# A graph and mixer network on one core: the second graph layer's projection in two column passes, with the attention columns in the first

## What is computed

```
xn = layernorm(x)
x  = x + gat2(elu(gat1(xn))) + mixer(xn)     # mixer ends in out @ proj_w.T + proj_b
x  = x + moe(layernorm(x))
```

```
h    = h1 @ W2                      # (1250 x 2048) @ (2048 x 768)
al_s = h . att_src2, al_d = h . att_dst2      # one number per node each
e    = leaky_relu(al_s[src] + al_d[dst]);  m = segment_max(e, dst)
ex   = exp(e - m[dst]);  out = segment_sum(h[src] * ex) / segment_sum(ex) + bias
```

## Time and profile before

| what | us |
|---|---|
| median of three runs | 2380.92 |
| the profiled execution | 2381.91 |
| its span, first to last instruction | 2380.1 |
| PE busy (88% of the span) | 2089.4 |
| DVE busy | 1112.9 |
| ACT busy | 414.8 |
| POOL busy | 202.4 |
| matmuls of the second layer's projection (L1337, x640) | 209.2 |
| mean granted TensorE clock | 0.927 |

### The profile page before, as it was taken

One profiled execution on the slowest core, in us unless ns is written; L12 is line 12 of the kernel. 1 busy time (PEld: TensorE's weight loads), 2 busy tenths in 40 slices (PEclk: granted clock), 3 DMA queues, 4 the chain that ended last, 5 costly groups with the idle time before them and its releaser, 6 DMA issues. The chain is left out here.

```text
span 2380.1 us, 33762 instructions
## 1 busy us (share of the span) xinstructions
PE 2089.4 (88%) x9786; PEld 1453.8 (61%) x9787; DVE 1112.9 (47%) x2372; ACT 414.8 (17%) x743; POOL 202.4 (9%) x197
## 2 busy tenths in 40 slices
PE   4998999889799994399999979975985799999997
PEld 2666666644345553288888845543554577777776
DVE  4113212422566665788888700117646333333433
ACT  1222121200011113122222200000000122222221
POOL 0000000000000001000000000000001123333322
PEclk9998999889899995599999989997996799999999
DMA  7002200142200007623333241182116488899664
GB/s 224 0 0 70 90 0 0 42 102 71 93 24 22 24 22 261 201 95 121 116 100 99 66 179 50 52 199 73 53 35 235 117 244 253 263 278 283 185 147 78
DMA packets 73572, 271.79 MB, mean 114 GB/s; under 512 B 10230, under 2 KB 26682, under 8 KB 63911
## 3 DMA queue, kind: packets, MB, share of 16 engines
q1 hardware_dynamic: 52263, 204.94, 26.3%
q0 software_dynamic: 14688, 54.19, 9.8%
q10 hardware_dynamic: 6560, 11.86, 1.3%
HBM read 208.95 MB, written 62.00 MB: 114 GB/s over the span
## 5 line engine op out<-in xcount | busy, mean ns | idle before, releaser
L1187 PE MATMUL gat_Z<-h,gat_wt 125*125 125x256 f32 (+1 forms) x1600 | 354.2, 380 | 20.5 <-DVE gat_wt L1103 20.5
L1187 PEld LDWEIGHTS gat_Z<-h,gat_wt 125*125 125x125 f32 x1600 | 297.6, 188 | 65.7 <-DVE gat_wt L1103 21.0
L552 PE MATMUL mix_G<-mix_w,mix_xs 128*125 128x384 f32 x720 | 243.5, 489 | 0.0
L835 PE MATMUL count_G<-gnn_w,xnT 128*125 (+1 forms) x480 | 214.8, 597 | 17.0 <-issue 17.0
L2004 PE MATMUL ex_PH<-ex_xT,ex_w 128*128 128x128 f32 x1872 | 224.0, 279 | 2.4 <-issue 0.9
L1337 PE MATMUL gat2p_Y<-gat2p_w,gat2p_hT 128*125 128x384 f32 x640 | 209.2, 491 | 12.1 <-DMA gat2p_w<-in_L_gnn_W 12.1
L2004 PEld LDWEIGHTS ex_PH<-ex_xT,ex_w 128*128 128x128 f32 x1872 | 215.0, 193 | 3.7 <-issue 3.7
L2014 PE MATMUL ex_PY<-ex_w,ex_hT 128*128 128x384 f32 x624 | 214.7, 494 | 1.2 <-ACT ex_hT L1953 1.0
L552 PEld LDWEIGHTS mix_G<-mix_w,mix_xs 128*125 128x125 f32 x720 | 133.4, 189 | 85.4 <-issue 3.1
L1337 PEld LDWEIGHTS gat2p_Y<-gat2p_w,gat2p_hT 128*125 128x125 f32 x640 | 121.3, 190 | 99.7 <-issue 14.8
L2014 PEld LDWEIGHTS ex_PY<-ex_w,ex_hT 128*128 128x128 f32 x624 | 114.3, 190 | 77.4 <-ACT ex_hT L1953 3.1
(11 more groups left out here) (291 smaller groups left out, 2321.7 us busy)
## 6 DMA issues: line engine op xcount, KB each, us to landing
ex_w<-in_L_ffn_W SPq DMA_DIRECT2D x64, 1152.0 KB, 9.1
gat_cnt<-c_dram SPq DMA_DIRECT2D x50, 546.9 KB
h1T_dram<-gat_oT ACTq DMA_DIRECT2D x40, 250.0 KB, 2.0
gat2p_hT<-h1T_dram SPq DMA_DIRECT2D x10, 1000.0 KB, 4.8
mix_w<-in_L_mix_qkv_w SPq DMA_DIRECT2D x6, 1152.0 KB, 12.5
ct_dram<-count_out SPq DMA_DIRECT2D x40, 157.0 KB, 2.1
mix_w_slice<-in_L_gnn_W SPq DMA_DIRECT2D x6, 1024.0 KB, 10.9
gat2p_w<-in_L_gnn_W SPq DMA_DIRECT2D x4, 1536.0 KB, 13.6
```

The costliest lines, as they stand in the source:

```text
L552: last = pe.matmul(G[c][:], xs[b][:, k, :], w[:, k, c, :], start=(k == 0), stop=(k == KD - 1))
L835: last = pe.matmul(G[t % 2][:], xnT[:, k, t * P:(t + 1) * P], w[:, k, bass.ds(hd * C1, C1)], start=(k == 0), stop=(k == KD - 1))
L1187: last = pe.matmul(Z[b][j][:], wt[b][:, s, :], h[:, s, bass.ds(hd, 1), j * HC:(j + 1) * HC + j], start=(s == 0), stop=(s == NT - 1))
```

## The change

In the output projection, SP loads, behind x, the two attention rows of the second layer and all of W2 (6144 KB, in four chunks) into their own tiles; DVE's loop is unrolled, and from tile 2 on DVE makes, after the copy for the tile two further on, four multiply-and-accumulates of 768 columns: two rows of 128 of W2 times the two attention vectors, 32 in all, into wa2 (128 x 16 x 2).

In the second layer's projection POOL copies wa2 into columns 384 and 385 of each of the 16 blocks of the weight tile. The work is 20 half-tiles, q = 0 to 19: first columns 0 to 385 for all ten tiles of nodes, then the other 384 columns for all ten. The tiles of h1T are thus loaded twice. W2 is loaded in eight chunks of 768 KB (1536 bytes per row), the four of the second pass one by one with the loads of q = 2 to 5; the mask is loaded tile by tile with q = 2 to 11, and x1 with q = 12. DVE evacuates the whole first pass, and al2 is a copy of two columns. ACT evacuates the second pass. The chain is woven in: PE transposes al2 after q = 10, and m after q = 15 (MAX_AT = 5). ACT, no longer SP, stores alT, waits for it, loads the two rows, and stores m. No loop is left in this phase.

```
+    a2_loaded, wa2_step = cx.sem("proj_a2_loaded"), cx.sem("proj_wa2_step")
+        w2s = sb(nc, st, "proj_w2s", [128, KF, D])
             rows_dma(sp, xr, x.rearrange("(t p) d -> p t d", p=P), x_loaded)
+            sp.dma_start(a2[:, 0, :], a_src2[0, :].partition_broadcast(128)).then_inc(a2_loaded, 16)
+            sp.dma_start(a2[:, 1, :], a_dst2[0, :].partition_broadcast(128)).then_inc(a2_loaded, 16)
+            for c in range(KF // KC):
+                sp.dma_start(w2s[:, c * KC:(c + 1) * KC, :],
+                             W2[c * KC * 128:(c + 1) * KC * 128, :].rearrange("(k p) n -> p k n", p=128)
+                             ).then_inc(w2_loaded[c], 16)
...
+            def attention_columns(k):
+                if k % KC == 0:
+                    dve.wait_ge(w2_loaded[k // KC], 16)
+                if k == 0:
+                    dve.wait_ge(a2_loaded, 32)
+                for s in range(2):
+                    n = 2 * k + s
+                    if n >= 2:
+                        dve.wait_ge(wa2_step, n - 1)
+                    dve.tensor_tensor_reduce(out=junk[:, s, :], in0=w2s[:, k, :], in1=a2[:, s, :], scale=1.0,
+                                             scalar=0.0, op0=ALU.mult, op1=ALU.add,
+                                             accum_out=wa2[:, k, s:s + 1]).then_inc(wa2_step, 1)
+
+            for t in range(NT):
+                add(t)
+                if t + 2 < NT:
+                    turn(t + 2, t % 2)
+                if t >= 2:
+                    for k in range(2 * (t - 2), 2 * (t - 1)):
+                        attention_columns(k)
...
+            load_h(0)
             for c in range(KF // KC):
+                load_w(0, c)
+            load_h(1)
+            for q in range(2, 2 * NT):
+                sp.wait_ge(projected, q - 1)
+                load_h(q)
+                if q - 2 < KF // KC:
+                    load_w(1, q - 2)
+                if q - 2 < NT:
+                    rows_dma(sp, mask[:, q - 2, :], mask_dram[q - 2, :, :], mask_loaded)
+                elif q - 2 == NT:
+                    rows_dma(sp, x1, x1_dram.rearrange("(t p) d -> p t d", p=P), x_loaded)
+
+        @block.gpsimd
+        def _(pool):
+            pool.tensor_copy(w[:, :, HW:W], wa2[:]).then_inc(ext_ready, 1)
...
             for t in range(NT):
+                dve.wait_ge(projected, t + 1)
+                dve.tensor_copy(h2[:, t, 0:HW], Y[t % 2][0][:, 0:HW]).then_inc(ev_first, 1)
+                dve.tensor_copy(al2[:, t, :], Y[t % 2][0][:, HW:W]).then_inc(ev_first, 1)
...
+            def evacuate(t):
+                act.wait_ge(projected, NT + t + 1)
+                act.activation(h2[:, t, HW:D], Y[t % 2][1][:, 0:HW], ACT.Copy).then_inc(ev_second, 1)
+
+            evacuate(0)
+            act.wait_ge(copied, 3)
+            act.dma_start(al2T_dram, alT[:]).then_inc(stored, 16)
+            act.wait_ge(stored, 16)
+            act.dma_start(row[:], al2T_dram[0, :].partition_broadcast(128)).then_inc(row_loaded, 16)
+            act.dma_start(rows_t[:], al2T_dram[1, :].partition_broadcast(128)).then_inc(rows_loaded, 16)
+            for t in range(1, MAX_AT + 1):
+                evacuate(t)
+            act.wait_ge(m_copied, 3)
+            act.dma_start(m2T_dram, mT[:]).then_inc(m_stored, 16)
+            for t in range(MAX_AT + 1, NT):
+                evacuate(t)
+            act.wait_ge(m_stored, 16)
...
+            def project(q):
+                t, j = q % NT, q // NT
+                b = t % 2
+                pe.wait_ge(in_loaded[q % 2], q // 2 * 16 + 16)
+                if t >= 2:
+                    pe.wait_ge(ev_second if j else ev_first, t - 1 if j else 2 * (t - 1))
+                cols = slice(j * W, j * W + HW) if j else slice(0, W)
                 for c in range(KF // KC):
+                    if t == 0:
+                        pe.wait_ge(w_loaded[j][c], 16)
+                    for k in range(c * KC, (c + 1) * KC):
+                        last = pe.matmul(Y[b][j][:, 0:HW if j else W], hT[q % 2][:, k, :], w[:, k, cols],
+                                         start=(k == 0), stop=(k == KF - 1))
                 last.then_inc(projected, 1)
 
+            pe.wait_ge(ext_ready, 1)
+            for q in range(NT + 1):
+                project(q)
+            pe.wait_ge(ev_first, 2 * NT)
             for j in range(3):
                 for t in range(width[j]):
                     last = pe.transpose(T[j][:, t, :], al2[:, 4 * j + t, :], ident[0:P, 0:P])
                 last.then_inc(turned, 1)
+            for q in range(NT + 1, NT + MAX_AT + 1):
+                project(q)
+            pe.wait_ge(copied, 3)
             pe.wait_ge(m_ready, 1)
...
+            for q in range(NT + MAX_AT + 1, 2 * NT):
+                project(q)
```

More of the change, by code:

```diff
@@ L310, in proj_phase @@
     biased = cx.sem("proj_biased")
+    a2_loaded, wa2_step = cx.sem("proj_a2_loaded"), cx.sem("proj_wa2_step")
+    KC = 4
+    w2_loaded = [cx.sem(f"proj_w2_loaded{c}") for c in range(KF // KC)]
     with ExitStack() as st:
+        w2s = sb(nc, st, "proj_w2s", [128, KF, D])
+        a2 = sb(nc, st, "proj_a2", [128, 2, D])
+        junk = sb(nc, st, "proj_junk", [128, 2, D])
         bias = sb(nc, st, "proj_bias", [128, 2, D])
@@ L1225, in gat2_project_phase @@
     dve_step = cx.sem("gat2m_step")
-    w_loaded = [cx.sem(f"gat2p_w{c}") for c in range(KF // KC)]
+    w_loaded = [[cx.sem(f"gat2p_w{j}{c}") for c in range(KF // KC)] for j in range(2)]
     in_loaded = [cx.sem(f"gat2p_in{b}") for b in range(2)]
-    HW = D // 2
     with ExitStack() as st:
-        w = sb(nc, st, "gat2p_w", [128, KF, D])
-        ab = sb(nc, st, "gat2p_a", [128, 2, D])
-        junk = sb(nc, st, "gat2p_junk", [P, 2, D])
+        w = sb(nc, st, "gat2p_w", [128, KF, D + 2])
+        junk = sb(nc, st, "gat2p_junk", [P, N])
         hT = [sb(nc, st, f"gat2p_hT{b}", [128, KF, P]) for b in range(2)]
@@ L1239, in gat2_project_phase @@
         mT = sb(nc, st, "gat2p_mT", [1, N])
-        Y = [[pb(nc, st, f"gat2p_Y{b}{j}", [P, HW]) for j in range(2)] for b in range(2)]
+        Y = [[pb(nc, st, f"gat2p_Y{b}{j}", [P, W]) for j in range(2)] for b in range(2)]
         T = [pb(nc, st, f"gat2p_T{j}", [2, 4, P]) for j in range(3)]
@@ L1256, in _ @@
[L1256 to L1272, removed]
+            def load_h(q):
+                sp.dma_start(hT[q % 2][:], h1T_dram[q % NT, :, :].rearrange("p (f d) -> p f d", d=P)
+                             ).then_inc(in_loaded[q % 2], 16)
@@ L1304, in _ @@
                     dve.wait_ge(maxed, t)
-                dve.tensor_tensor_reduce(out=mjunk, in0=row[0:P, :], in1=mask[:, t, :], scale=1.0, scalar=-3.0e38,
+                dve.tensor_tensor_reduce(out=junk[:], in0=row[0:P, :], in1=mask[:, t, :], scale=1.0, scalar=-3.0e38,
                                          op0=ALU.subtract, op1=ALU.max, accum_out=big[:, t:t + 1]).then_inc(maxed, 1)
             dve.wait_ge(maxed, NT)
+            dve.wait_ge(ev_first, 2 * NT)
             step(dve.tensor_tensor(big[:], big[:], al2[:, :, 1], ALU.add))
@@ L1324, in _ @@
+            for t in range(MAX_AT + 1, NT):
+                evacuate(t)
+            act.wait_ge(m_stored, 16)
         @block.tensor
         def _(pe):
[L1326 to L1331, removed]
-                for c in range(KF // KC):
[L1333 to L1338, removed]
-                last.then_inc(projected, 1)
@@ L1341, in _ @@
[L1341 to L1345, removed]
-            pe.wait_ge(al_step, 2 * NT)
+            def project(q):
[5 more added lines that the diff above has]
+                cols = slice(j * W, j * W + HW) if j else slice(0, W)
+                for c in range(KF // KC):
+                    if t == 0:
[3 more added lines that the diff above has]
+                                         start=(k == 0), stop=(k == KF - 1))
+                last.then_inc(projected, 1)
```

58 lines of the change are left out of this document (19 added, 39 removed).

## The result

| | before | after |
|---|---|---|
| median (lowest to highest) | 2384.1 (2375.8 to 2401.9) | 2375.3 (2354.7 to 2383.6) |
| runs | 20 | 20 |
| profiled execution, span | 2381.9, 2380.1 | 2375.3, 2373.5 |

The ratio of after to before is 0.9924, with a 95% interval of 0.9904 to 0.9943: faster by 0.76%, some 18 us. The means differ by 16.2 us (2387.6, 2371.4), the medians by 8.8. These don't agree because neither kernel has one time. Of the 20 runs after, 7 lie at 2354.7 to 2365.8 (median 2360.3) and 13 at 2373.9 to 2383.6 (2376.2); of the 20 before, 14 at 2375.8 to 2389.2 (2383.8) and 6 at 2395.8 to 2401.9 (2397.4). Upper group against upper group the change brings 21 us, lower against lower 24. The forecast, 2355.0 with a range of 2346 to 2364, had the direction right; the time is 20 us above it and outside its range.

What follows compares the result with a forecast made beforehand. PE, busy 88% of the span, was taken as the bound, with gaps around the second projection. Terms -32.6 - 1.5 + 0.5 + 5.5 + 1.5 + 0.6 = -26.0 us gave 2355, range 2346 to 2364.

Steps and rivals of the forecast that it cites:

- PE's clock doesn't enter: Start of the aggregation: PE meets it after 10.5 us idle instead of 11.9, so no clock term was added.
- end gap: Between the second projection's last matmul and the aggregation: hiding the chain cuts 45.57 us of gap, saving 32.6 us.
- start: Start of the second projection: a smaller first chunk of W2 lets PE begin earlier, -1.5 us.
- two columns: Two extra columns in the first pass's matmuls and the aggregation's first half: 0.5 us, plus 0 for the loads, taken +0.5.
- wait for tile 13: First pass, q = 13: h1T's tile 13 queues behind x1, PE waits 1.3 to 9.4 us, taken +5.5.
- clock behind it: After the wait at q = 13, PE's clock drops and the next instructions run slower, +1.5 us.
- output projection: End of the output projection: DVE's last reductions delay the logits, +0.6 us (0 to 3.6); x's wait unchanged.
- B: Rival, second projection: x1 is not in the way, tile 13 lands in time; -33 us, 2348; chance 0.22.
- D: Rival: reading h1T twice makes loads bound both passes, slower than before, 2415 at 130 GB/s; chance 0.05.
- P: Rival, output projection: x shares bandwidth evenly with W2 and comes 9.4 us later, 2364; chance 0.06.
- a wait for x above 11 us: Sign that would prove the forecast wrong: PE's wait for x in the output projection, then 10.79 us, growing.
- C: Rival, second projection: the first pass waits for loads at q = 2 to 5, 8 us, 2363; chance 0.12.

Runs made afterwards that it cites:

- e5: Changed kernel with ACT's store of al2 and its broadcast row loads moved behind the evacuations of tiles 0 to 2; 2358.5 us, one run.
- e1: Kernel before with ten spare matmuls filling PE's idle time ahead of the norm-and-routing phase; 2385.6 us, ratio 0.9976.
- e7: Changed kernel with SP waiting for x in the output projection before loading the attention rows and W2; 2373.7 us, one run.
- e8: Changed kernel with the whole chain (both transposes, ACT's store and loads) behind the last half-tile, so not hidden; 2391.4 us, one run.
- e9: Changed kernel with x1 loaded by tile, W2 loaded only after x has landed, reductions one tile earlier; 2348.7 us, ratio 0.9824.
- e2: Changed kernel with the same ten spare matmuls as e1 ahead of the norm; 2368.3 us, ratio 0.9901.
- e10: Same three edits on the changed kernel as e9, plus the ten spare matmuls of e1; 2344.9 us, ratio 0.9818.
- e6: Changed kernel with only x1's last 13 partitions loaded two tiles later, with q = 14; 2357.8 us, one run.

## Why the prediction was wrong

**The step that failed** is the sum itself: its six terms are all of the touched phases, and every other phase stands in it at nothing, without a reason. "Nothing outside these phases is touched" was taken to mean that nothing outside them moves; "PE's clock doesn't enter" was said of the aggregation alone, and no sentence asks for the clock of the norm. I summed the change against one execution of before and took it to be the same kernel in all else. Its norm phase had its clock back at 1.00 after some 3 us; that of the profiled execution after never had: +13.6 us, the largest term of the difference after the hidden chain. That such a price was possible could have been read before the change: the trace of before has the norm's first matmuls at 0.50, behind 8.6 us of idle time. The three times given for before (2379.93 to 2384.01) all lie in its lower group, so nothing shown had the second one. They were also low within it: the 20 runs of before have a median of 2384.1, 3.2 us above the 2380.9 that I started from.

**The difference of the profiled spans**, 2373.5 - 2380.1 = -6.6, adds up: start of the output projection -1.5 (473.1 against 474.6; from 100 to 220 us the mean granted clock is 0.94 before and 0.99 after), output projection +3.0, up to the second projection -0.4, its start -1.8, projection -20.9, aggregation +1.5, norm +13.6, the rest -0.1. The touched phases bring -19.7 where I had -26.0. Term by term (the six add up to -19.1; 0.6 us are not placed):

| term | forecast | measured | from |
|---|---|---|---|
| end gap | -32.6 | -32.1 | PE idle 10.99, not 10.51 |
| start | -1.5 | -1.8 | 7.21 us from load to matmul, was 9.00 |
| two columns | +0.5 | +0.5 | tile to tile 10.37 us in the first pass, 10.32 in the second |
| wait for tile 13 | +5.5 | +9.4 | 9.42 |
| clock behind it | +1.5 | +1.9 | 12.40 - 10.32 - 0.17 |
| output projection | +0.6 | +3.0 | below |

**The wait** was the right mechanism at the wrong size, at the very end of its bounds (1.3 to 9.4). I had the rows at 0 to 5.6 us, and e5 shows 4.8. Without them the sum left 1.3 to 3.8 us, and e5 still waits 4.6: x1, taken at the mean of its first load, has a piece of 13 partitions that I had not priced apart, and issuing it later takes 5.9 us off. On the rule that the DMA engines take turns between queues ("DMA: Bandwidth & Descriptors", "Queues, rings and completion order", in the Trainium skill) the trace agrees: ACT's small store landed 5.9 us after its issue while x1's 3.84 MB were still moving in SP's queue, both rows landed before tile 13, and taking the rows out of that time took 4.8 us off the wait. B (tile 13 in time) and D are out.

**The output projection** is P in small. x doesn't keep its place ahead of W2, but what it loses is not half the bandwidth: PE restarts 27.6 us after the phase's first load, not 25.9, and the wait is 12.5 against 10.8 (+1.7), the 24 matmuls behind it 10.31 against 9.44 (+0.9), and the reductions at the end, from the last add's end to the logits, 581.86 - 578.04 = 3.8 against 3.4 (+0.4; the prediction's own times, 580.9 and 580.41, give +0.5, not +0.6). The sign that I had named, a wait for x above 11 us, came true, but it was a poor one: e1 has 12.0 without any load of W2 there. I took 0 from a load of x whose followers behind it I counted as proof; that row had no run without them to stand against. e7 takes away 2.9 of the 3.0.

**Right by the runs:** m's transposes in their slot (no wait of PE there), ACT's and DVE's work hidden, no wait for W2 in the first pass (C), and a slower projection if the chain were not hidden (e8). In e9's profile the touched phases bring +0.3 - 1.8 - 32.4 = -33.9, what I had worked out for B (-33), and its time is 2348.7, B's 2348. That the times agree so closely is luck: the profiled execution with these phases took 2355.7. In the lower group the kernel as changed takes 2360.3, inside the range and 5 us above the forecast. The wait with the clock behind it and the output projection are 6.7 us more than I had; that they are those 5 is not shown.

**Open:** why PE's clock comes back in the norm in one run and not in another, whether the change shifts how often it does, and what moves the start of the output projection by up to 10 us. The aggregation is 1.5 us longer in the three profiles with a slow norm (135.3) than before, but 135.2 in e1 as well, with a fast one.

## What to carry to other kernels

Before summing a change against one profile, look for phases where PE starts light work out of an idle time at the low clock, and ask what the sum would be if the clock didn't come back: here one such phase was worth 13.6 us, two thirds of what the edited phases brought. A bulk load put into a queue ahead of a just-in-time load should be cut into pieces as large as the slack between two tiles, and a remainder on few partitions priced by itself: spreading x1 gained 11.5 us, a third of the 32 at the end of the projection. A gain is read in the touched phases first and in the total second.

## What the runs showed of the hardware that was not expected

- A phase whose PE is busy all the time stayed at 1.2 GHz from its first matmul at 1757.19 to its end at 1794.14, 37 us. Its work is matmuls of 36 columns and transposes of 125. In six other profiles the same phase began at 1.2 GHz too and was back at 2.4 some 3 us later (in before between 1778 and 1781). Begun at 2.4 GHz, behind spare matmuls, it stayed there (e1, e2, e10). Projections with 384 columns came back within one tile (12.4 us, then 10.3).
- While 13 partitions of x1, 0.40 MB, moved, the DMA engines were busy at a low rate: share 1.18 and 0.94 at 128 and 126 GB/s in after, with the end of a broadcast row beside them, and 0.73 at 89 GB/s in e6, against 388 and 395 for tile 13.
- Loads queued behind another in the same queue still delayed it: from the phase's first load to PE's restart on x were 27.1 to 27.6 us with W2 behind it (seven profiles), 25.2 to 25.9 without (five).
- A store of 10 KB took 1.5 us to landing where no other load moved (e8), and 5.9 and 6.6 beside large loads.
